# Layer 1's weight splits, angles and distance tables made in layer 0's last batch, and layer 0's tail taken tile by tile

## The reference

```
x  = x + L0_attn(layernorm(x)) * silu(L0_ffn(layernorm(x)))   # layer 0
x  = x + L1_attn(layernorm(x)) * silu(L1_ffn(layernorm(x)))   # layer 1
L0_attn: 8 heads, two score maps each over the 512 tokens of a batch,
         att = softmax(map 0) - diff_weight * softmax(map 1); rms norm; Wo
L0_ffn : top-2 of 8 experts over a rank-16 compression
L1_attn: q, k, v = x @ W_in.T + b_in, 16 heads of 64, attention over axis 0 (length 8); scores and values with embeddings of the clipped distance (k_dist, v_dist); W_out
L1_ffn : real = x @ cos(theta + noise); imag = x @ sin(phi + noise); sqrt(real^2 + imag^2)
```

## Time and profile before

| | |
|---|---|
| time, median of 3 runs | 1354.02 us (1349.83 to 1356.14) |
| profiled execution | 1348.0 us, its span 1346.2 us |
| mean granted TensorE clock | 0.958 of full |
| TensorE busy | 1224.7 us (91%) |
| VectorE, ScalarE, GpSimd busy | 957.1, 680.0, 604.7 us |
| last exp of layer 0 ends | 657.3 us |
| all engines enter layer 1's block | 692.0 us |
| first V matmul, and end of the last | 712.2 and 723.3 us |

### The profile page before, as it was taken

How to read it: one execution, slowest core, us unless ns; L and a number is a source line. 1 busy time by engine, 2 the same in 40 slices (tenths; PEclk the granted TensorE clock), 3 DMA queues, 4 the chain that set the end, 5 groups by cost and what they waited for, 6 DMA issues and landing times. The chain is left out here.

```text
span 1346.2 us, 30256 instructions
## 1 busy us (share of the span) xinstructions
PE 1224.7 (91%) x10752; PEld 771.5 (57%) x10752; DVE 957.1 (71%) x2084; ACT 680.0 (51%) x1293; POOL 604.7 (45%) x618
## 2 busy tenths in 40 slices
PE   3889999999999999898769899999999999999997
PEld 2333344444444444343358687777878777786875
DVE  2766776777778777776375968688696868869675
ACT  2356666666665666666343344344344434434442
POOL 2165667676766767766642313132231313223131
PEclk8598999999999999999869999999999999999999
DMA  4634453554444354450240010010101001010000
GB/s 125 145 80 88 98 117 88 118 119 93 99 91 106 87 126 91 99 117 8 99 175 32 3 47 3 10 41 1 49 2 49 2 10 41 1 49 2 32 3 17
DMA packets 57205, 86.27 MB, mean 64 GB/s; under 512 B 8064, under 2 KB 38016, under 8 KB 56832
## 3 DMA queue, kind: packets, MB, share of 16 engines
q1 hardware_dynamic: 57088, 84.58, 25.8%
HBM read 50.47 MB, written 33.55 MB: 62 GB/s over the span
## 5 line engine op out<-in xcount | busy, mean ns | idle before, releaser
L821 DVE TENSOR_REDUCE negmax<-s_bank 128x1 f32<-128x512 f32 x512 | 330.9, 680 | 76.2 <-PE s_bank L555 75.7
L969 POOL TENSOR_TENSOR room<-room 128x512 f32<-128x512 f32 x256 | 318.8, 1276 | 130.2 <-ACT room L685 130.2
L685 ACT ACTIVATE room<-t_bank 128x512 f32<-128x512 f32 x512 | 284.8, 597 | 79.7 <-PE t_bank L565 74.5
L555 PE MATMUL s_bank<-kst,qst 48*128 48x512 f32 x512 | 214.1, 488 | 15.6 <-DMA kst<-park 13.4
L565 PE MATMUL t_bank<-qst,kst 50*128 50x512 f32 x512 | 207.0, 468 | 17.0 <-ACT room L685 12.8
L565 PEld LDWEIGHTS t_bank<-qst,kst 50*128 50x128 f32 x512 | 83.6, 188 | 140.2 <-ACT room L685 82.0
L1724 POOL TENSOR_TENSOR room<-rt,apart 128x512 f32<-128x512 f32 x32 | 42.2, 1339 | 234.6 <-DVE rt L1533 234.6
L578 PE MATMUL a_bank<-room,v 128*32 128x512 f32 x1024 | 137.6, 611 | 0.2
L1709 POOL TENSOR_TENSOR ex<-ex,rc 128x256 f32<-128x256 f32 x64 | 41.9, 655 | 188.6 <-DVE rc L1561 188.6
L1576 DVE STREAM_TRANSPOSE pt<-ex 32x256 f32<-32x256 f32 x256 | 111.0, 434 | 10.1 <-POOL ex L1709 3.6
L1262 PE MATMUL pr<-xt_h,win_h 128*128 128x512 f32 x256 | 105.6, 413 | 0.0
(11 more groups left out here) (251 smaller groups left out, 2282.1 us busy)
## 6 DMA issues: line engine op xcount, KB each, us to landing
park<-qk_h SPq DMA_DIRECT2D x128, 128.0 KB, 2.4
qst<-park SPq DMA_DIRECT2D x64, 192.0 KB, 3.8
kst<-park SPq DMA_DIRECT2D x64, 192.0 KB, 4.3
park<-qk_l SPq DMA_DIRECT2D x64, 128.0 KB, 2.4
room<-in_x SPq DMA_DIRECT2D x8, 512.0 KB, 4.5
xr<-in_x SPq DMA_DIRECT2D x8, 512.0 KB, 5.3
xb<-x SPq DMA_DIRECT2D x8, 512.0 KB, 4.4
xr<-x SPq DMA_DIRECT2D x8, 512.0 KB, 3.7
```

Of the source, the lines that this page charges most:

```text
L555: pe.matmul(s_bank[S_BANK[w]][:, :], qst[slot][rows, j, c * P:(c + 1) * P], kst[slot][rows, j, :], start=True, stop=True).then_inc(m.s_don ...
L685: act.activation(probs[:, c, j, :], t_bank[w % 2][:, :], ACT.Exp, scale=SCALE0).then_inc(m.exp_done, 1)
L821: dve.tensor_reduce(negmax[:, i_par, 2 * odd + j, c:c + 1], s_bank[S_BANK[w]][:, :], X, ALU.max, negate=True).then_inc(m.max_done, 1)
L969: add = pool.tensor_tensor(sums[:, pair, h, :], probs[:, 2 * pair, h, :], probs[:, 2 * pair + 1, h, :], ALU.add)
```

## The change

Its parts, as the code makes them:

- **Memory.** W_in gets a buffer of its own (`win`), so it can be loaded while `probs` is in use. The split weights `win_h` and `win_l` lie over the stacks `qst`, `kst` and over `xt`, `xt_h`, `xt_l`, `wqk_h`, `wqk_l`, which batch 7 doesn't need any more at that point.
- **Loads.** In batch 7 SyncE issues six loads of W_in after the first job M, and ten small ones (tables, angles) after the second; `vdx` and `wout` come in the tail. As soon as the first x1 tile of batch 7 is stored, SyncE loads layer 1's first tokens (`load_tokens`), and it no longer waits for the other stores at the end of the block.
- **Last batch.** ScalarE gets six roundings of W_in (`HIGH`), VectorE six subtractions (`LOW`), 15 steps of the angles (`TRIG`) and eight small products (`KDB`), and TensorE the two table products, GK at (2, 9) and BETA at (2, 13), through `misc`.
- **Tail.** The last half's denominators take the exp tiles directly, four steps (`last_denominators`), without GpSimd's pairs. ZT comes first, TD after two TA; the maps are added tile by tile (`add_last_maps`).
- **Layer 1.** The work that is done once is gone but for the sines, and R stands behind two V jobs in the first tile.

```diff
+TRIG = ((2, 9), (2, 10), (2, 11), (2, 12), (3, 0), (3, 1), (3, 2), (3, 3), (3, 4), (3, 7), (3, 9), (3, 11), (3, 12),
+        (3, 13), (3, 14))
+HIGH = ((1, 10), (1, 12), (2, 4), (2, 8), (3, 2), (3, 6))
+LOW = ((2, 6), (2, 7), (2, 13), (2, 14), (3, 8), (3, 10))
+KDB = (2, 8)
+LAST_SLOTS = (((2, 9), "GK", B - 1, 0), ((2, 13), "BETA", B - 1, 0))
...
+    def high_weights(self, act, n):
+        if n == 0:
+            act.wait_ge(self.w_load, 16 * 3 * KC)
+        part, k = PARTS[n // KC], n % KC
+        act.activation(self.win_h[part][:, k, :], self.win[:, k, part * H1 * D1:(part + 1) * H1 * D1],
+                       ACT.Copy).then_inc(self.w_high, 1)
...
+            def last_denominators(c):
+                pe.wait_ge(m.exp_done, HALF * UNITS * B - UNITS + 4 * c + 4)
+                for h in range(HG):
+                    mm = pe.matmul(d_bank[BLK * h:BLK * h + BLK, :], pick[:, HALF - 1, :], probs[:, c, h, :],
+                                   start=False, stop=(c == 3))
...
+                            if last and hf == HALF - 1 and w >= 7:
+                                last_denominators(w // 4 - 1)
...
-            sp.wait_ge(m.xt_psum, KC * B)
-            shared.load_first(sp, io1)
             sp.wait_ge(m.ta_psum, QT * B)
             shared.load_last(sp, io1)
-            for t in range(QT):
+            for t in range(2):
                 store_x1(B - 1, t)
-            for stored in m.x1_stored:
-                sp.wait_ge(stored, 16 * B * QT // 2)
+            sp.wait_ge(shared.x1_stored_even, 16 * (QT // 2) * (B - 1))
+            sp.wait_ge(shared.x1_stored_first, 16)
+            shared.load_tokens(sp, x1_dram)
+            for t in range(2, QT):
+                store_x1(B - 1, t)
...
-            add_pair(B - 1, 3, 1)
-            add_maps(B - 1)
+            for k in range(QT):
+                add_last_maps(k)
...
+                    if first and (kind, k) == ("V", 2):
+                        distances(i)
```

More of the change, by code:

```diff
@@ L224, in less_turns @@
[L224 to L227 removed]
+        elif op:
+            dve.wait_ge(self.trig, step)
+        if op == 0:
+            dve.tensor_tensor(ang, ang, turns, ALU.add).then_inc(self.trig, 1)
+        if op == 1:
+            dve.tensor_scalar(turns, ang, float(1 / (2 * np.pi)), ROUND, ALU.mult, ALU.add).then_inc(self.trig, 1)
@@ L434, in store_x1 @@
                 stand_alone(sp, m.sp_passed)
-                sp.dma_start(x1_dram[t * P:(t + 1) * P, b, :], x1_tile(b, t)).then_inc(m.x1_stored[t % 2], 16)
+                stored = shared.x1_stored_first if isinstance(b, int) and (b, t) == (B - 1, 0) else m.x1_stored[t % 2]
+                sp.dma_start(x1_dram[t * P:(t + 1) * P, b, :], x1_tile(b, t)).then_inc(stored, 16)
             sp.wait_ge(m.ones, HALF)
@@ L530, in job @@
                 if kind == "OT":
-                    pe.wait_ge(m.o_ok, i + 1)
+                    pe.wait_ge(m.o_ok, B - 1 + QT if isinstance(i, int) and i >= B - 1 else i + 1)
                     for t in range(QT):
@@ L581, in value_step @@
                 mm.then_inc(m.a_done, 1)
+            def last_denominators(c):
[3 more added lines that the diff above has]
+                                   start=False, stop=(c == 3))
+                if c % 2:
+                    mm.then_inc(m.d_done, 1)
+                else:
+                    stand_alone(pe, m.pe_passed)
             def denominators(b, hf, pair):
-                first, last = (hf, pair) == (0, 0), (hf, pair) == (HALF - 1, PAIRS - 1)
+                first = (hf, pair) == (0, 0)
+                last = (hf, pair) == (HALF - 1, PAIRS - 1) and not (isinstance(b, int) and b >= B - 1)
                 if first:
@@ L656, in _ @@
             over_batches(pe, body, 2, 2)
-            for step in range(16 - LAG, 16):
-                value_step(B - 1, step // 4, step % 4)
-            for pair in range(PAIRS):
-                denominators(B - 1, HALF - 1, pair)
+            last_denominators(3)
+            value_step(B - 1, HALF - 1, 3)
             wait(pe, *drained(*prev))
@@ L712, in side @@
                 if kind == "SQ":
-                    act.wait_ge(m.o_ok, i + 1)
+                    act.wait_ge(m.o_ok, i + 1 + (k if isinstance(i, int) and i >= B - 1 else 0))
                     if k == 0:
@@ L1043, in body @@
                 gated(b)
-                add_pair(b, 3, 0)
+                if not last:
+                    add_pair(b, 3, 0)
                 if not (isinstance(b, int) and b >= B - 2):
@@ L1113, in layer1 @@
         ec = sb("ec", [P, 2, 2, TT, NREL])
[L1114 removed]
+        pt = shared.pt
         ot = shared.ot
@@ L1313, in body @@
                 prev_misc[0] = ("R", i, 0)
+            def body(i):
+                last = isinstance(i, int) and i >= NT1 - 1
+                first = isinstance(i, int) and i == 0
+                if not isinstance(i, int):
+                    prev_misc[0] = ("PD", i - 1, 0)
+                if not first:
+                    distances(i)
+                pe.wait_ge(m.xt_low, KC * (i + 1))
                 for kind, k in steps:
+                    if first and (kind, k) == ("V", 2):
+                        distances(i)
                     if isinstance(i, int) and i == 0 and (kind, k) == ("Q", 0):
-                        pe.wait_ge(m.w_low, 3)
+                        pe.wait_ge(m.u_load, 16 * shared.U_LOADS)
+                        pe.wait_ge(m.xt_low, KC)
                         for hp in range(HP):
```

326 lines of the change are left out of this document (192 added, 134 removed).

## The result

The changed kernel takes 1371.9 us (median of 4, 1369.4 to 1374.0) against 1351.9 for the kernel before (4 runs, 1347.4 to 1356.1), 1.0147 times as long (95% interval 1.0107 to 1.0188). So it is 1.5% slower, clear of the noise, where I had forecast 1346.5 and at worst 1357. The last exp comes at 677.9, beyond the 672 that I had named as the sign of being wrong. The profiled execution has a span of 1367.5 against 1346.2. This is where its 21.3 us lie; the marks are rows of the two timelines (ScalarE's evacuation in unit (0, 10) of the last batch, the last exp, the first operation of layer 1's block, and the first R record of each token tile).

The account below looks back on a forecast made before the run. TensorE was taken to be held by the tail's and layer 1's chains of waits and half-speed once-only work. Saving 16.8 us (containing the tail's 10.0) less batch 7's 9.2 gave 7.6: median 1346.4, written 1346.5, range 1340 to 1357.

Parts of the forecast that it names:

- Part 1: Batch 7, the last: the added side jobs cost 9.2 us, between 5.5 if ScalarE's work hides and 14.2 if nothing does.
- so GK costs about 3.5 at full clock: Last batch: GK's 16 matmuls, 6.98 us at half clock, would take about 3.5, counted as 3.3.
- GK and BETA: Last batch, TensorE's table products: 3.3 us for GK and 1.5 for BETA, less than their lengths because ScalarE has work queued.
- Roundings at (2, 4), (2, 8), (3, 2), (3, 6): Last batch, ScalarE: (2, 4) costs 1.0 us, (2, 8) and (3, 2) 0, (3, 6) shares 1.0 with the first denominator step.
- Roundings at (1, 10), (1, 12): Last batch, ScalarE: two roundings of 1.06 us each, four units apart with ZT between, cost 1.5 for both.
- Angles and low halves on VectorE: Last batch: subtractions, angle steps and small products, 18 us, fit VectorE's idle time and cost 0.
- Loads: Last batch, SyncE: W_in, issued after 602.6, lands before the exp starting at 620.2, some 3 us to spare; cost 0.
- Rival C: Last batch: weights land late, ScalarE's first rounding blocks the exps, up to 18 us late, 1364; chance 0.12.
- Part 2: Layer 0's tail: first WF job 7.0 us earlier, layer 1's block start at 682.0 instead of 692.0, 10.0 earlier.
- Part 3: Layer 1's first tile: V and R end at 706.5 instead of 723.3, 16.8 us earlier; 1.65 lost to low clock.
- Nothing else in the eight tiles moves: Layer 1's token tiles beyond the first tile's gain: no change, 0 us.
- Rival B: Last batch: VectorE and GpSimd exclude each other, WF comes 6.6 us late, saving 1.0, 1353; chance 0.21 together with D.

Follow-up runs that it names:

- round6_out: Changed kernel, shifted by 16 increments, all six roundings and low halves moved to layer 0's tail, GK and BETA left in the last batch: 0.9995 of the kernel before.
- gk_out: Changed kernel, shifted by 16 increments, GK and BETA moved from the last batch to layer 1's start: 1352.1 us, 1.0008 of the kernel before.
- wide_fill: round6_out with GK's and BETA's matmuls replaced by 7 and 4 of 256 columns, 70 increments: 62.2 us from (0, 10) to the last exp.
- after_pad48: Changed kernel plus 48 TensorE semaphore increments at layer 1's start, nothing else: 1357.0 us, 1.0019 of the kernel before.
- gk_round6_out: Changed kernel, shifted by 16 increments, GK and BETA at layer 1's start, all six roundings and low halves in layer 0's tail: 1347.3 us, ratio 0.9969.
- after_pad8: Changed kernel plus 8 TensorE semaphore increments at layer 1's start, nothing else: 1377.1 us, 1.0151 of the kernel before.
- before_pad37: Kernel before plus 37 TensorE semaphore increments at layer 1's start, nothing of the change: 1372.0 us against 1354.6, ratio 1.0130.
- tail_all: Changed kernel, shifted by 16 increments, GK, BETA, six roundings and low halves spread over layer 0's tail where engines wait: 1339.2 us against 1351.9, ratio 0.9894.
- after: The changed kernel itself, without added increments: 1371.9 us against 1351.9 for the kernel before, ratio 1.0147.

## Why the prediction was wrong

**What bounds the kernel:** right as read, but incomplete. It looked at each stretch for busy engines and waits. Neither thing that cost time can be read there: where the loop's head lies in the instruction stream, and what narrow matmuls (16 columns for each load of weights) do to the clock of what follows.

**Part 1, the last batch: 9.2 forecast, 19.1 measured.** The failing step is the phrase "so GK costs about 3.5 at full clock".
- GK and BETA: 4.8 forecast, 9.5 to 9.8 measured. With wide matmuls of the same nominal length it was 62.2 less 56.0 less 1.7, 4.5: the length (3.75 at full clock in round6_out) and its place on the path were right, and the step that priced it took the clock as given. What it left out is the clock of the work behind. A hint was in the earlier trace rows, since GK stood in the stretch at clock 0.51, but I put that down to the waits around it.
- Roundings at (2, 4), (2, 8), (3, 2), (3, 6): 1.0 and what (3, 6) shares; with their low halves they measured 5.2 to 5.5. The wait at (2, 4) was 0.93, as forecast. In gk_out 2.16 more was VectorE's (see below), and the rest goes with a second stretch of low clock right behind that wait. Whether the later three would hide under TensorE's work at full clock, as I argued, was not tried one by one.
- Roundings at (1, 10), (1, 12): 1.5 forecast, 0.8 to 0.9 measured.
- Denominators: 1.9 forecast, 1.7 measured.
- Angles and low halves on VectorE: 0 forecast, and this 0 was wrong too. A subtraction took 1.65 to 1.75 where I had 1.12, and in gk_out the gate came late behind two of them and TensorE waited 2.16. In the changed kernel, where TensorE itself is slow there, that wait doesn't show. Twelve of the fifteen angle steps cost nothing that could be measured. The 0.89 ahead of BETA isn't VectorE being late: it had itself waited 6.41 for ScalarE, and BETA waits until the WF job before it has been read out of `misc`; the 0.89 stands in wide_fill too.
- Loads: no hole on ScalarE before the first rounding, at 622.20. The last was issued by 607.5, and they took 8.8 us in the median from issue to landing, so they were in time. Rival C, which rested on the 96 GB/s of the earlier trace rows, didn't happen; the stretch was slower for other reasons.

**Part 2, the tail:** block start 23.5 after the last exp (24.7 forecast, 34.7 before), first WF job 12.3 after it (13.5 forecast). Right.

**Part 3, layer 1's first tile:** V 10.2 after the block's start (10.0), V and R done after 26.0 (24.5). V's first 5.9 us ran at half clock, which loses 2.9; I had taken "half of 3.3, 1.65", and the 3.3 stands in no row (R had taken 3.65). Right in mechanism, 1.5 too short.

**"Nothing else in the eight tiles moves": wrong by 16.8 us,** the costliest sentence, and one for which I had looked at no row. The five cuts are 11.2 of it, the two stretches of low clock behind them some 4 (83.0 and 83.1 against 80.7 to 81.2), and 1.5 stays without any cut: in after_pad48 it is 472.2 from R of the second tile to R of the eighth, and 471.7 to 472.7 in the other kernels without a cut that carry the change. Of that 1.5 I know no cause.

**Rival B** (VectorE and GpSimd shut each other out) accounts for part of gk_out's 2.16 us, and not for what is left with all low halves and nearly all angles gone, 59 to 60. It also showed where I hadn't put it, in the tail of gk_round6_out, as above. There the rule of the Trainium skill ("SBUF — State Buffer", section "SBUF: two separate sides") agrees with the trace: a product of GpSimd's that began beside a subtraction took 1.71 instead of 0.72. **Rivals A and D** were variations of size, and too small.

The sum, put right: the forecast -7.6, +9.9 in the batch, -1.2 in the tail, +1.6 in the first tile, +16.8 and +0.3 in the others, and 1.5 that lie ahead of the change, make 21.3.

## What to carry to other kernels

A change to the code ahead of a long loop can shift the loop over a block boundary of the instruction stream: look for an idle stretch with no releaser at the same instruction of each iteration but the first, count the instructions between the loop's head and that place, and shift it by a few increments in a waiting stretch. Price a side job by what it does to the clock of the work behind it: narrow matmuls cost twice over in a stretch that was at full clock, and little in a gap (the tail grew by 1.2 us in all). A moved piece of work should go where its own engine waits and the engine that it would slow waits too; behind the last exp there was room for nearly all of it.

## What the runs showed of the hardware that I hadn't expected

- After the loop's backward branch the block of instructions behind that of the loop's head is there about 3 us after the head starts (2.57 to 3.38 over fifteen iterations of three kernels); with 24 records between nothing is seen of it, with five it costs 1.85 to 2.51 us in each iteration, with one 2.42 to 3.07. The packet appears 0.2 to 0.6 us after the head (three tiles looked at); why the instructions are usable only some 2.5 us later stays open.
- Two of the five pauses of the changed kernel, the two longest (2.51 and 2.50), were followed by a stretch at 1.2 GHz, and those iterations were 2 us longer than the others. The length of the pause doesn't decide it: in after_pad8 the clock fell behind 2.42 and 2.66 and not behind 2.67, 2.70 and 3.07, in before_pad37 behind 1.98 and not behind 2.01.
- 32 records of 16 columns (3.64 us in tail_all, 3.75 in round6_out, TensorE busy throughout) were followed by a clock of 1.2 GHz for most of the next 4 us; 14 records of 256 columns in nearly the same time were not.
- 48 increments in a waiting queue delayed what stood behind them by 1.2 us.
- The same code can keep or lose the clock from one execution to the next: after, after_pad48 and after_pad8 have the same last batch, and only after_pad8 has a stretch of low clock 17 us behind (0, 10).
